# First two LoRA evictions side by side, a W1 load on the other queue, and the threshold setup moved in a four-layer conditional kernel

## The reference

```python
x = x + x @ w_eff.T              # L0: w_eff = quantized(weight + delta) + delta, delta = 0.5 * lora_B @ lora_A (rank 64)
x = x + x @ W.T + 2 * lora_out   # L1: top-2 gate over 8 experts of rank 16, with a language bias on the logits
x = x + x @ W.T + b + 2 * lora   # L2: one of 24 adapters of rank 16 for each batch row
x = x + x @ w[adapter_ids].T     # L3: one of 16 full 1024 x 1024 weights for each batch row
```

## Time and profile before

| What | Value |
|---|---|
| Median of 3 runs | 672.22 us (671.55 to 672.97) |
| The profiled execution: its time | 672.67 us |
| its span, first to last instruction | 670.9 us |
| PE busy | 664.2 us, 99% of the span |
| DVE busy, ACT busy | 352.7 us (53%), 280.3 us (42%) |
| POOL busy | 90.1 us (13%) |
| PE clock granted | 1.000 of full speed |

### The profile page before, as it was taken

How to read it: one execution, slowest core, us unless ns; L and a number is a source line. 1 busy time by engine, 2 the same in 40 slices (tenths; PEclk the granted TensorE clock), 3 DMA queues, 4 the chain that set the end, 5 groups by cost and what they waited for, 6 DMA issues and landing times.

```text
span 670.9 us, 9316 instructions
## 1 busy us (share of the span) xinstructions
PE 664.2 (99%) x3308; PEld 571.1 (85%) x3308; DVE 352.7 (53%) x540; ACT 280.3 (42%) x420; POOL 90.1 (13%) x120
## 2 busy tenths in 40 slices
PE   8999999999999999999999999999999999999997
PEld 7889999999999988888889888888888888888886
DVE  5799899879951374215644123661421653421453
ACT  6764665952722361204552123553121563120453
POOL 2130225005010030001210000220000211000120
PEclk9999999999999999999999999999999999999999
DMA  9653111001000503003874001776000686000372
GB/s 293 195 176 95 32 45 50 1 1 63 1 1 0 189 21 130 0 1 109 297 219 151 0 0 47 262 236 229 0 0 0 198 291 210 16 0 1 107 230 102
DMA packets 39442, 67.07 MB, mean 100 GB/s; under 512 B 3572, under 2 KB 23284, under 8 KB 39412
## 3 DMA queue, kind: packets, MB, share of 16 engines
q1 hardware_dynamic: 34340, 58.28, 26.6%
q10 hardware_dynamic: 5072, 8.39, 3.7%
HBM read 58.27 MB, written 8.39 MB: 99 GB/s over the span
## 4 chain that ended last, share of the span: by engine, by line
PE 93%; DVE 3%; DMA 1%; ACT 1%; SPq 1%; issue 0%; POOL 0%; ACTq 0%; DVEq 0%; POOLq 0%
PE ps L1069 29%; PE ps L1071 29%; PE ps L1070 29%; PE ps L1204 3%; PE ps L1206 1%; PE ps L1237 1%; DMA w_w<-w 1%; DVE tmp L852 1%; DVE e_both L781 1%; PE ps L1080 1%; ACT tmp L585 0%; DVE w_w L848 0%; DVE w_w L842 0%; DVE ring_lo L781 0%; PE ps L1245 0%
## 5 line engine op out<-in xcount | busy, mean ns | idle before, releaser
L1069 PE MATMUL ps<-e_both,ring_hi 128*128 128x384 f32 (+3 forms) x384 | 133.8, 348 | 1.3 <-ACT raw L557 0.6
L781 DVE TENSOR_TENSOR ring_lo<-raw,ring_hi 128x512 fp32r<-128x512 f32 x128 | 91.4, 726 | 82.0 <-ACT ring_hi L689 81.9
L1071 PE MATMUL ps<-e_both,ring_lo 128*128 128x384 f32 (+3 forms) x384 | 133.3, 347 | 0.0
L689 ACT ACTIVATE ring_hi<-raw 128x512 fp32r<-128x512 f32 x128 | 79.4, 629 | 70.3 <-PE ps L1071 66.0
L1069 PE MATMUL ps<-ring_hi,e_mid 128*128 128x512 f32 x264 | 102.4, 388 | 0.0
L1071 PE MATMUL ps<-ring_hi,e_mid 128*128 128x512 f32 x264 | 102.3, 388 | 0.0
L1070 PE MATMUL ps<-ring_lo,e_mid 128*128 128x512 f32 x264 | 102.3, 388 | 0.0
L1069 PE MATMUL ps<-x_both,e_both 128*128 128x512 f32 x256 | 101.5, 397 | 0.0
L1070 PE MATMUL ps<-x_both,e_both 128*128 128x512 f32 x256 | 101.2, 395 | 0.0
L1071 PE MATMUL ps<-x_both,e_both 128*128 128x512 f32 x256 | 101.0, 394 | 0.0
L527 POOL TENSOR_TENSOR raw<-raw,ident 128x128 f32<-128x128 f32 x64 | 39.3, 616 | 319.7 <-DMA raw<-w_t 319.7
(11 more groups left out here) (154 smaller groups left out, 859.0 us busy)
## 6 DMA issues: line engine op xcount, KB each, us to landing
raw<-w_t SPq DMA_DIRECT2D x64, 512.0 KB, 3.7
xraw<-x_t SPq DMA_DIRECT2D x16, 512.0 KB, 4.6
y<-tmp ACTq DMA_DIRECT2D x30, 256.0 KB, 3.5
w_w<-w SPq DMA_DIRECT2D x14, 512.0 KB, 4.0
e_both_w<-w_t SPq DMA_DIRECT2D x5, 512.0 KB, 9.1
e_both_w<-w_t SPq DMA_DIRECT2D x4, 384.0 KB, 6.6
e_mid_w<-bs SPq DMA_DIRECT2D x24, 64.0 KB, 2.9
w_w<-w SPq DMA_DIRECT2D x3, 256.0 KB, 7.0
```

Of the source, the lines that this page charges most:

```text
L689: act.activation(ring_hi[:, (2 * k + h) % 4, :], raw[:, k % RAW, h * 512:(h + 1) * 512], ACT.Copy).then_inc(w3_hi, 1)
L781: return dve.tensor_tensor(out, whole, hi.bitcast(F32), ALU.subtract)
L1069: pe.matmul(out, a[0], b_[0], start=start, stop=False, **kw)
L1071: return pe.matmul(out, a[1], b_[0], start=False, stop=stop, **kw)
```

## The change

Five edits, all in the order of work; no instruction of computation is added or removed.

1. In the plan the second `delta` comes ahead of `("w1_first", 1)`.
2. The load of W1's tile 1, k = 4 to 7 (256 KB), goes from the fourth place in SP's queue to the third in ACT's.
3. `("thr",)` stands ahead of `("br", 0)` and `("w2", 1, 3)`, where it stood behind both.
4. One round goes from before `("br", 2)` to the section m = 12 (W0's tile 4, 150 us later).
5. With that, all rounds between the two places come one round earlier in number.

```diff
-ROUNDS_FIRST = 8
-ROUNDS_IN = {2: 5, 3: 4, 4: 5, 5: 4, 6: 4, 7: 0, 8: 2, 9: 5, 10: 5, 11: 5, 12: 1}
+ROUNDS_FIRST = 7
+ROUNDS_IN = {2: 5, 3: 4, 4: 5, 5: 4, 6: 4, 7: 0, 8: 2, 9: 5, 10: 5, 11: 5, 12: 2}
...
-    plan = [("lora_first",), ("w1_first", 0), ("w2", 0, W2_ORDER[0][0]), next(early), ("w1_first", 1), next(early)]
+    plan = [("lora_first",), ("w1_first", 0), ("w2", 0, W2_ORDER[0][0]), next(early), next(early), ("w1_first", 1)]
...
-    plan += [("f", 0), ("f", 1), next(early), ("w2", 1, 2), next(early), ("br", 0), ("w2", 1, 3)]
-    plan += [("thr",), ("lora",)] + list(early) + [("w2", 2, 0)] + some(2) + [("f", 2), ("as",)]
-    plan += some(2) + [("br", 1)] + some(1) + [("f", 3)] + some(1) + [("w1", 2), ("f", 4)] + some(2) + [("br", 2)]
-    plan += some(0) + [("f", 5)]
+    plan += [("f", 0), ("f", 1), next(early), ("w2", 1, 2), next(early), ("thr",), ("br", 0), ("w2", 1, 3)]
+    plan += [("lora",)] + list(early) + [("w2", 2, 0)] + some(2) + [("f", 2), ("as",)]
+    plan += some(2) + [("br", 1)] + some(1) + [("f", 3)] + some(1) + [("w1", 2), ("f", 4)] + some(1) + [("br", 2)]
+    plan += [("f", 5)]
...
             load_w2(sp, 0, W2_ORDER[0][0])
-            load_w1_first(sp, 1)
             load_w2(sp, 0, W2_ORDER[0][1])
...
             load_w1_first(act, 0)
+            load_w1_first(act, 1)
```

## The result

| | before | changed |
|---|---|---|
| Median (range), us | 672.22 (671.55 to 672.97), 7 runs | 674.53 (674.14 to 675.09), 7 runs |
| Ratio, 95% interval | 1 | 1.0034 (1.0023 to 1.0046) |
| The profiled execution: time / span, us | 672.67 / 670.9 | 674.50 / 672.7 |
| PE busy / DVE busy, us | 664.2 / 352.7 | 665.1 / 353.8 |

The change costs 2.3 us in the medians, 1.8 us between the two profiled executions. The forecast was 673.0 in a range up to 674.0, so the time lies outside it, on the slow side.

A forecast was written before the change was run, and what follows sets the result against it. PE's own work was taken to bound the kernel after its last wait at 49.87 us. Edit 3's net 0.59 and the front's 0.2, other edits zero, gave +0.8 us: 673.0 against the median of 672.22, range 671.7 to 674.0.

The forecast's parts named there:

- What bounds the kernel: PE's own work after its last wait at 49.87 us; changes behind 50 us cannot gain, only lose.
- Edits 4 and 5, zero: Moved round of two DVE instructions, hidden in 6.61 us of DVE idle before W0's tile 6 at 201.06: zero.
- some 2 us: Cost of the moved round if DVE's idle cover before W0's tile 6, at 201.06 us, were gone.
- Edit 3 and chunk 6, +1.17 and -0.58: Earlier thresholds make PE wait at chunk 2's k = 6, +1.17 us; chunk 6's wait at 49.87 goes, -0.58: net +0.59.
- a front 0.39 late: DVE's third W2 piece ends at 16.03, 0.39 us late; half, 0.2, passes to DVE's piece (1, 2).
- Edit 1, nothing: Chunk 0 begins 0.52 us earlier, but PE waits longer for the third W2 piece: 0.0, at worst +0.5.
- Edit 2, +0.2: Load on ACT's queue makes W2's first piece 0.36 us late; the front's 0.39 passes on by half, 0.2.
- It lies 0.45 above the median: Profiled execution before, 672.67 us, against median 672.22; so 673.5 expected for that execution became 673.0 against the median.
- a whole overtaking, 0.72: W2's first piece 0.72 us later if the 256 KB load goes wholly ahead of it; the middle bound.
- The bound of 1.6 us: Upper bound for W2's first piece's lateness, 256 KB at 163 GB/s; rival of 674.4 us at this bound, chance 0.20.
- The sum: 0.59 for edit 3 and 0.2 for the front: +0.8 us, 673.0 against the median of 672.22.
- if a wait turns up behind 50 us: Sign named as showing the forecast wrong: any PE wait after 50 us, where it expected none.

The follow-up runs named there:

- the split thresholds: Kernel before with the Exp and the first 9 of the 20 threshold instructions moved ahead of br 0 and piece (1, 3): 671.54 us, again 671.67.
- the load ahead on SP's own queue: Kernel before with W1's 256 KB load (tile 1, k = 4 to 7) issued ahead of W2's first piece on SP's queue: 672.44 us, ratio 1.0001.

## Why the prediction was wrong, and where it was right

**What bounds the kernel: right, and then not followed.** "Nothing that the change does behind 50 us can gain; it can only lose, by making a wait where there is none." It did just that at 109.17. The prediction looked for hidden gates up to 50 us, where "a semaphore is checked without a wait", and not behind it.

**Edits 4 and 5, zero: the step that failed.** "In between, DVE's work comes earlier, never later, and PE has no wait there to lose. Zero". Both halves are wrong. W1's low parts come earlier, but the rounds come later against PE, by one round, 2.5 us (DVE ends the second pair at 108.43 and not at 105.04, and 0.87 of that is PE's own lateness). And PE has a gate on the rounds there, with 1.7 us of cover. The cost is 0.95 in the trace of all, 0.88 with these edits alone. That the wait is due to the rounds' place is shown from three sides: edits 4 and 5 alone make it, putting the round back ahead of it takes it away, and asking for product 14 later takes it away too. The price named for lost cover, "some 2 us", belonged to another place (201 us) and another mechanism. The row that would have told was in the trace: ACT idle for 9.33 us at 105.13, waiting for line 861. An engine that stands still for 9 us waiting for the work that is about to be delayed has to be asked who waits for it.

**Edit 3 and chunk 6, +1.17 and -0.58: right.** In the trace of all edits PE's lateness grows by 1.19 at k = 6 and shrinks by 0.57 at chunk 6. PE was to go on at 29.45 + 0.2 = 29.65 and did at 29.68, but there luck helped. The 0.2 was half of a front 0.39 late. The front was 0.25 late at the third piece, and nearly all of it passed: ACT's split of piece (1, 2) begins at 21.51 instead of 21.28, 0.23 later. The front was taken too late in the profiled execution and its passing on too small, and the two errors cancel. The net, 0.59, measured 0.62 in the trace of all and 0.70 in the medians of edit 3 alone.

**Edit 1, nothing: right for edit 1 by itself.** The third piece comes 7.2 to 7.3 us after the first split in either order. Beside edit 2 it is not quite nothing: edit 2 alone has 7.01, and both together 7.26.

**Edit 2, +0.2: the mechanism likely right, the term too small.** The forecast had the piece 0.36 late and half of the front passed on. By the estimates of the last column the piece is 0.66 late, and nearly all of it passes. Against the profiled execution before, which is what the sum was made against, the front is only 0.25 late at the third piece, close to what was said, and that hides the error. It comes out in the step from that execution to the median. "It lies 0.45 above the median" was taken off the sum as though it were scatter that would be the same in the changed kernel. It was most likely the late landing itself: its first split began at 8.44, while others of the kernels with the load on SP's queue began as early as 7.29 to 7.82, and the split thresholds, at 8.36, also took 0.50 more than their median. The executions with the load on ACT's queue begin in that late range every time, so the 0.45 is not to be taken off. In the medians edits 1 and 2 cost 0.79, or 1.33 - 0.70 = 0.63 on top of edit 3, where the 0.23 at chunk 6 has no wait to show in.

The price that the prediction had for a whole overtaking, 0.72, stands near the 0.6 estimated for the load ahead on SP's own queue; the median of that kernel, +0.23, hides it, since the early load saves 0.32 behind the split. The bound of 1.6 us rested on the 163 GB/s of one execution: in the same stretch the seven other executions that issue the load behind the piece moved 0.40 to 0.53 MB, 202 to 266 GB/s. The prediction said that the trace of before has no moment at which both queues carry large loads side by side. It has one, from 3 to 4 us, and SP's queue got 0.03 MB of 0.28 there. The Trainium skill, "DMA: Bandwidth & Descriptors", section "Queues, rings and completion order", has engines take turns between rows that have work, by which the piece would be slowed in part when the load comes from the second queue. The traces agree in direction: the piece is late with the load on ACT's queue, by 0.66 in the estimate. They do not show the part, since the load wholly ahead of the piece costs the same within the error of these estimates.

**The sum.** In medians: front 0.6 to 0.8, thresholds 0.7, round 0.9, together 2.2 to 2.4, against 2.31 measured and 0.8 forecast. Of the 1.5 us missing, some 0.9 are the round, some 0.5 the front and 0.1 the thresholds.

**What would have shown it wrong** was named, "if a wait turns up behind 50 us", and that is what happened.

## What to carry to other kernels

When a list of background work is shortened at one place, everything behind it in the list is late against the engine that sets the pace until the item comes back. Follow the last item of each batch to whoever waits for it, and measure that cover before you cost the move at nothing; gates without a wait are found in the code and in long idle times of other engines, not in the list of waits. Before you subtract the distance of a profiled execution from its median, find what made it: if it is one late transfer, ask whether the change fixes that transfer late or early. A long chain of small instructions can be cut where the gap ends, and the half that fits may bring the gain that the whole could not.

## What the runs showed that I had not expected

The landing of the very first large transfers scatters by over 1 us between executions that issue them alike: 7.74 to 8.80 for the first split in the six that issue the piece at 2.24 or 2.25 and the load behind it. In the kernel with two traces it passes to the end of 670 us undiminished, because PE hardly waits afterwards. Most of the scatter of a kernel's runs, 0.8 to 1.7 us between lowest and highest, can be that alone. And so one trace is not enough to price a load that overtakes: 8.24, with 256 KB put ahead of the first piece on the same queue, looked like no cost, until the kernel's median and the 0.32 saved behind the split were set beside it.
